# A graph network layer on one core: gathering rows of h in three bf16 parts instead of rows of a first-layer table

## The reference

```python
h = jnp.maximum(_layernorm(x, axis=-1), 0.0)
# layer 0: an MLP over every edge in both directions, summed at the nodes
x_p, x_f = h[src], h[dst]
fwd = concatenate([x_f, x_p, edge_attr], axis=1)      # 80 wide
bwd = concatenate([x_p, x_f, edge_attr], axis=1)
m = relu(concatenate([fwd, bwd]) @ Wf1 + bf1) @ Wf2 + bf2
flow = segment_sum(m, concatenate([dst, src]))         # 64 wide
x = x + relu(flow @ Wn1 + bn1) @ Wn2 + bn2
# layer 1: sum of neighbours
h = jnp.maximum(_layernorm(x, axis=-1), 0.0)
return x + segment_sum(h[dst], src)
```

## Time and profile before

| | |
|---|---|
| median of 3 runs | 9138.04 us |
| profiled execution: span, first to last instruction | 7224.1 us |
| profiled execution: its own time | not given apart from the span |
| start, up to POOL's first gather | 149.8 us |
| edge phase, first gather to last scatter | 149.8 to 4323.8 us |
| busy: POOL, TensorE, VectorE, ScalarE | 5197.9, 4419.8, 3200.3, 1352.3 us |
| mean granted TensorE clock | 0.624 |
| moved by the DMA queue of POOL's DMAs | 183.68 MB in 153824 packets |

### The profile page before, as it was taken

One profiled execution on the slowest core, in us unless ns is written; L12 is line 12 of the kernel. 1 busy time (PEld: TensorE's weight loads), 2 busy tenths in 40 slices (PEclk: granted clock), 3 DMA queues, 4 the chain that ended last, 5 costly groups with the idle time before them and its releaser, 6 DMA issues.

```text
span 7224.1 us, 127054 instructions
## 1 busy us (share of the span) xinstructions
PE 4419.8 (61%) x23241; PEld 3987.8 (55%) x23244; DVE 3200.3 (44%) x15358; ACT 1352.3 (19%) x4288; POOL 5197.9 (72%) x5767
## 2 busy tenths in 40 slices
PE   4666666666666666666666679999733333333333
PEld 3655556555555655555565569999533333333333
DVE  5444444444444444444444466666523232323232
ACT  2222222222222222222222234434200000000000
POOL 2777777777777777777777766666377777777776
PEclk8666676666766666766667785555655555555555
DMA  5222222222222222222222123333111111111111
GB/s 154 43 46 43 43 43 43 43 42 43 42 43 43 42 43 42 42 42 42 43 42 42 41 35 73 71 71 73 30 14 14 14 14 14 14 14 14 14 14 20
DMA packets 1109393, 290.45 MB, mean 40 GB/s; under 512 B 992782, under 2 KB 1058701, under 8 KB 1108518
## 3 DMA queue, kind: packets, MB, share of 16 engines
q0 software_dynamic: 153824, 183.68, 10.7%
q1 hardware_dynamic: 954758, 88.54, 10.3%
q10 hardware_dynamic: 576, 16.16, 0.7%
HBM read 223.49 MB, written 82.32 MB: 42 GB/s over the span
## 4 chain that ended last, share of the span: by engine, by line
POOL 59%; issue 27%; DVE 6%; PE 3%; DVEq 2%; DMA 2%; POOLq 0%; ACT 0%; ACTq 0%; SPq 0%
POOL records L620 21%; POOL ring L674 20%; POOL ring L610 18%; DVE acc L1266 3%; DVEq L331 1%; PE bank L1010 1%; DVE oht L1337 1%; DVE ohd L1337 1%; DVEq L1266 1%; DMA ring<-records 0%; PE bank L943 0%; PE bank L846 0%; DMA row_next<-in_sd 0%; PE bank L944 0%; PE bank L972 0%
## 5 line engine op out<-in xcount | busy, mean ns | idle before, releaser
L620 POOL DMA_INDIRECT records<-rec,pos x1664 | 1650.3, 992 | 526.7 <-issue 507.8
L674 POOL DMA_INDIRECT ring<-h_rows,didx x1568 | 1491.1, 951 | 576.3 <-issue 477.5
L610 POOL DMA_INDIRECT ring<-t_rows,sidx x1568 | 1519.5, 969 | 484.9 <-issue 482.1
L943 PE MATMUL bank<-ring,ident 128*128 x3328 | 1094.3, 431 | 1254.6 <-DMA ring<-t_rows,sidx 1249.8
L943 PEld LDWEIGHTS bank<-ring,ident 128*128 128x128 f32 x3328 | 868.4, 320 | 1309.9 <-issue 1309.8
L1072 PE MATMUL bank<-ring,ohd 128*128 x1664 | 376.2, 402 | 1282.8 <-POOLq L684 1282.2
L1072 PEld LDWEIGHTS bank<-ring,ohd 128*128 128x128 f32 x1664 | 362.9, 330 | 1295.9 <-issue 1295.9
L1275 DVE TENSOR_TENSOR prod<-bank,q_row 128x392 f32<-128x392 f32 x416 | 235.7, 567 | 1895.8 <-PE bank L959 1895.6
L944 PE MATMUL bank<-w,cmb 113*128 113x128 f32 x3328 | 1026.2, 411 | 0.0
L1266 DVE TENSOR_TENSOR acc<-acc,bank 128x65 f32 x3328 | 734.6, 221 | 524.9 <-issue 279.1
L1266 DVE TENSOR_TENSOR xs<-xs,bank 128x32 f32 x1664 | 304.3, 183 | 1384.2 <-PE bank L1072 1371.3
(11 more groups left out here) (213 smaller groups left out, 6508.9 us busy)
## 6 DMA issues: line engine op xcount, KB each, us to landing
ring<-records SPq DMA_DIRECT2D x104, 536.0 KB, 4.3
rec_i<-by_d_sd SPq DMA_DIRECT2D x1664, 1.0 KB
cmb<-by_d_ea SPq DMA_DIRECT2D x1664, 8.0 KB
records<-rec,pos POOLq DMA_INDIRECT x1664
ring<-t_rows,sidx POOLq DMA_INDIRECT x1568
ring<-h_rows,didx POOLq DMA_INDIRECT x1568, 2.4
by_d_ea<-in_ea ACTq DMA_DIRECT2D x8, 1579.0 KB, 19.1
t_rows<-cmb SPq DMA_DIRECT2D x26, 256.0 KB, 2.2
```

The lines of the kernel that those rows point to most:

```text
L610: nc.gpsimd.indirect_dma_start(out=ring[:, m * W + r * U + u, :], out_offset=None, in_=t2_rows, in_offset=bass.IndirectOffsetOnAxis(ap=sid ...
L620: nc.gpsimd.indirect_dma_start(out=records, out_offset=bass.IndirectOffsetOnAxis(ap=pos[:, r, u:u + 1].bitcast(U32), axis=0), in_=rec[:, r ...
L674: nc.gpsimd.indirect_dma_start(out=h2g[:, w * W + t, :], out_offset=None, in_=h2_rows, in_offset=bass.IndirectOffsetOnAxis(ap=didx[:, k, t ...
L943: nc.tensor.matmul(p, ident[:, :], ring[:, bass.ds(at[u], 1), :].rearrange("p a c -> p (a c)"), start=True, stop=False)
```

## The change

The table is no longer made. In its place ScalarE's three bf16 parts of h are written to DRAM as they are (`h3_rows`, 96 bf16 numbers a row, 192 bytes; one DMA). POOL gathers those rows. TensorE turns each gathered tile by a product with the identity (`transpose_sources`, four bf16 products a group), ScalarE copies the result (one more copy of 96 x 512 a group) into the first 96 rows of `cmb`, the expanded dst parts go to a buffer of their own (`cmb_dst`), and `hidden` is now `wdst` times `cmb_dst` plus `wsrc` times `cmb`, both fp32. The wait for the gather moves from `hidden` to `transpose_sources`, which stands half a group earlier. Gathers run LEAD = 4 groups ahead, and a gather stands behind the scatter of its step. In the start the table products leave TensorE's stream, h's parts are made earlier, one of the three reads of each piece of the schedule moves from VectorE to ScalarE, and the second is done once for all four pieces. POOL's first gather no longer waits for the schedule.

```diff
-ring = ring_flat.rearrange("p (t c) -> p t c", c=P)
+hring = ring_flat[:, 0:RG * H3 // 2].bitcast(BF16).rearrange("p (t c) -> p t c", c=H3)
+cmb_dst = rest[0:H3, 0:2 * U * P].rearrange("p (k u n) -> p k u n", k=2, u=U)
@@ SyncE @@
-            rounds_of(sp, NG // 2, store_t2)
-            sp.wait_ge(sched_done, 1)
...
+            load_sources(0, 0)
+            load_sources(1, 1)
+            sp.wait_ge(hi_ready, 1)
+            sp.wait_ge(mid_ready, 1)
+            sp.wait_ge(lo_ready, 1)
+            sp.dma_start(h3_rows.rearrange("(b p) f -> p b f", p=P), h3[:, :, :]).then_inc(h3_written, 16)
+            sp.wait_ge(sched_done, 1)
+            sp.wait_ge(ea_first, 16)
@@ GpSimd @@
-            for k in range(2):
-                pool.wait_ge(t2_written[k], 16 * (NG // 2))
             pool.wait_ge(rearranged, 1)
             nc.gpsimd.memset(cmb[H3:H3 + 1, :, :, :], 1.0).then_inc(ones_set, 1)
-            pool.wait_ge(mid_ready, 1)
             pool.wait_ge(hist_ps, 2)
-            pool.wait_ge(sched_done, 2)
+            pool.wait_ge(h3_written, 16)
...
-                        out=ring[:, m * W + r * U + u, :], out_offset=None, in_=t2_rows,
+                        out=hring[:, m * W + r * U + u, :], out_offset=None, in_=h3_rows,
...
-                        m2, r2 = m + (r + 2) // R, (r + 2) % R
+                        m2, r2 = m + (r + LEAD) // R, (r + LEAD) % R
+                        scatter_records(s * 8 + m, r)
                         if m2 < gathers:
-                            gather_t2(s + m2 // 8, m2 % 8, r2)
-                        scatter_records(s * 8 + m, r)
-            gather_t2(0, 0, 0)
-            gather_t2(0, 0, 1)
+                            gather_h3(s + m2 // 8, m2 % 8, r2)
+            for g in range(LEAD):
+                gather_h3(0, g // R, g % R)
@@ ScalarE @@
-            tables(0, True, False)
             nc.scalar.activation(h3[:, :, 0:D], h, ACT.Copy).then_inc(hi_ready, 1)
-            span(act, 1, 8, tables)
             act.wait_ge(r1_ready, 1)
-            nc.scalar.activation(h3[:, :, D:2 * D], ln_tmp, ACT.Copy).then_inc(mid_ready, 1)
-            span(act, 8, NG // 2 - 1, tables)
+            nc.scalar.activation(h3[:, :, D:2 * D], h, ACT.Copy).then_inc(mid_ready, 1)
...
+                    nc.scalar.activation(base_row[k][:, c * JC:(c + 1) * JC], pb[6][:, 0:JC], ACT.Copy).then_inc(base_copied, 1)
...
+                act.wait_ge(srcT_ps, v)
+                nc.scalar.activation(cmb[0:H3, r, :, :].rearrange("p u n -> p (u n)"), pb[5][0:H3, :], ACT.Copy)
                 act.wait_ge(hd_ps, v)
-                nc.scalar.activation(cmb[0:H3, r, :, :].rearrange("p u n -> p (u n)"), pb[1][0:H3, :], ACT.Copy).then_inc(cmb_ready, 1)
+                nc.scalar.activation(cmb_dst[:, r % 2, :, :].rearrange("p u n -> p (u n)"), pb[1][0:H3, :], ACT.Copy).then_inc(cmb_ready, 1)
@@ TensorE @@
+            def transpose_sources(i, r, gathered):
+                at = four(pe, gs_row, i * W + r * U, RG - 1)
+                if gathered:
+                    pe.wait_ge(gat[r], 16 * U * (i + 1))
+                for u in range(U):
+                    ins = nc.tensor.matmul(pb[5][0:H3, u * P:(u + 1) * P], hring[:, bass.ds(at[u], 1), :].rearrange("p a c -> p (a c)"), ident_h[:, :],
+                                           start=True, stop=True)
+                ins.then_inc(srcT_ps, 1)
...
-                    nc.tensor.matmul(p, ident[:, :], ring[:, bass.ds(at[u], 1), :].rearrange("p a c -> p (a c)"), start=True, stop=False)
-                    ins = nc.tensor.matmul(p, cmb[:, r, u, :], w3[:, :], start=False, stop=True)
+                    nc.tensor.matmul(p, cmb_dst[:, r % 2, u, :], wdst[:, :], start=True, stop=False)
+                    ins = nc.tensor.matmul(p, cmb[:, r, u, :], wsrc[:, :], start=False, stop=True)
@@ VectorE @@
+            dve.wait_ge(hi_ready, 1)
+            nc.vector.tensor_tensor(h, h, h3[:, :, 0:D], ALU.subtract).then_inc(r1_ready, 1)
             digit_one_hots(0)
+            dve.wait_ge(mid_ready, 1)
+            nc.vector.tensor_tensor(h, h, h3[:, :, D:2 * D], ALU.subtract).then_inc(r2_ready, 1)
             digit_one_hots(1)
...
-                    nc.vector.tensor_copy(base_row[k][:, s], pb[6][:, 0:JC])
-                    nc.vector.tensor_scalar(blk[k][:, s], pb[6][0:1, 0:JC], 1.0 / P, None, ALU.mult)
                     nc.vector.tensor_copy(e0f[:, s], pb[7][0:1, HCOL:HCOL + JC]).then_inc(sched_read, 1)
+                dve.wait_ge(base_copied, (n + 1) * (J // JC))
+                own.link(nc.vector.tensor_scalar(blk[k][:, :], base_row[k][0:1, :], 1.0 / P, None, ALU.mult))
```

More of the change, by code:

```diff
@@ L447, in _ @@
             sp.wait_ge(h2_written, 16)
-            for k in range(2):
-                sp.wait_ge(t2_written[k], 16 * (NG // 2))
+            sp.wait_ge(h3_written, 16)
         FB_STEPS = 15
@@ L833, in _ @@
             pe.wait_ge(wflow_ready, 1)
-            def transpose_h(i, k):
-                pe.wait_ge(hs_ready, i * 2 + k + 1)
-                nc.tensor.transpose(pb[k][:, 0:P], hs[:, k, :], ident[:, :]).then_inc(hsT_ready, 1)
-            def tables(i, first, last):
-                for k in range(2):
-                    if not first:
-                        pe.wait_ge(t2s_ready, i * 2 + k - 1)
-                        pe.sem_inc(pe_tick, 1)
-                    pe.wait_ge(hT_ready, i * 2 + k + 1)
-                    for u in range(U):
-                        ins = nc.tensor.matmul(pb[2 + k][:, u * P:(u + 1) * P], hT[:, k, :], w12[:, u, :], start=True, stop=True)
-                    ins.then_inc(tab_ready, 1)
-                if not last:
-                    for k in range(2):
-                        transpose_h(i + 1, k)
             def tile_counts(k):
@@ L879, in _ @@
             nc.tensor.matmul(pb[7][0:NB, 481:482], ident[0:NB + 1, 1:NB + 1], start_col[:, :], start=True, stop=True).then_inc(n_ready, 1)
-            tables(5, False, False)
             tile_counts(1)
-            tables(6, False, False)
-            schedule(1, 0)
-            schedule(1, 1)
-            tables(7, False, False)
-            schedule(1, 2)
-            schedule(1, 3)
-            tables(8, False, False)
+            for c in range(J // JC):
+                schedule(1, c)
             pe.wait_ge(hexp_ready, 1)
@@ L891, in _ @@
                              start=True, stop=True).then_inc(ncol_ps, 1)
-            tables(9, False, False)
             pe.wait_ge(ncol_ready, 1)
@@ L896, in _ @@
             nc.tensor.matmul(pb[7][0:NB, 481:482], upto[0:NB, 0:NB], ncol[:, :], start=True, stop=True).then_inc(n_ready, 1)
-            tables(10, False, False)
             tile_counts(0)
-            tables(11, False, False)
-            schedule(0, 0)
-            schedule(0, 1)
-            tables(12, False, True)
-            schedule(0, 2)
-            schedule(0, 3)
-            pe.wait_ge(t2s_ready, NG)
+            for c in range(J // JC):
+                schedule(0, c)
             q = pb[4][:, 0:(U + 1) * NB].rearrange("p (u b) -> p u b", b=NB)
@@ L1477 @@
     x[0:N] = inputs["x"]
-    w12 = np.zeros((P, U, P), np.float32)
-    for u in range(U):
-        w12[u * D:(u + 1) * D, u, :] = np.concatenate([second, first], axis=1)
-    as_dst = np.concatenate([first, second], axis=1)
+    as_src, as_dst = np.concatenate([second, first], axis=1), np.concatenate([first, second], axis=1)
     twice = np.concatenate([w["bf1"], w["bf1"]])[None, :]
```

133 lines of the change are left out of this document (52 added, 81 removed).

## The result

Five runs of the changed kernel had a median of 9222.14 us (9186.49 to 9224.75), beside 9138.04 us for before (five runs, 9119.58 to 9163.98). The ratio is 1.0075 [1.0052, 1.0097]: 0.75% slower, where 9108 us was predicted with 0.14 for "slower".

What follows compares the result with a forecast made beforehand. POOL's stream of indirect DMAs was taken to bound the edge phase. Steady state 0, start -36 and last groups +6 gave -30 us, from 9138 to 9108 us, own range 9065 to 9167 us (9060 to 9170 us stated with the chances).

Steps and rivals of the forecast that it cites:

- What bounds the kernel now: Edge phase: POOL's stream of indirect DMAs fills it, 10.3 us a group; TensorE's 3.2 us wait for gathers is slack.
- the sum: Whole kernel: 0 - 36 + 6 = -30 us; span 7194 us, median 9108 us, the 1913.9 us outside the span unchanged.
- Part 1: Edge phase, steady state: added products and copy stay under POOL's 10.3 us a group, so they cost nothing.
- TensorE's round: Edge phase: 7.1 us a group without its wait, 7.7 us with the products, 8.3 us with the copy too.
- TensorE was the bound: Rival, edge phase: the wait at L943 is true loss, round falls 10.3 to 8.3 us, 8324 us; chance 0.03.
- dearer gathers: Rival, edge phase: gathers into a bf16 ring cost POOL more, each 10 ns adding 16 us; 9190 us, chance 0.12.
- The price of a gather: POOL, edge phase: 192-byte bf16 rows cost the present 969 ns, change 0; ends -18 and +23 ns, -28 and +36 us.
- Part 2, the start: Start of the kernel: first scatter at 136.4 instead of 167.62 us, four more gathers behind it; gain 36 us (25 to 45).
- The eight pieces of the schedule: Start, VectorE: 1.6 us each, 12.8 us plus twice 1.0 us, instead of 28.9 us; saves 14.1 us.
- that step: Start: without table products in TensorE's stream VectorE goes on at 87.5 us, 9.1 us earlier (bounds 7 and 13).
- Part 3, the last groups: Last 24 groups, without gathers: products partly show and the last gathered group is further back, +6 us (0 to +18).
- The rule of the Trainium skill: DMA of rows under 512 bytes: less than full rate, gathers' data later, but POOL free as soon and the sum unchanged.

Runs made afterwards that it cites:

- after_c: The changed kernel (after), unchanged, run again on an occasion without pauses: 7213.12 us, 0.9985 [0.9975, 0.9994] of before; profile span 7209.6 us.
- before_again: The kernel before, unchanged, profiled once more: 9133.96 us, with a span of 9132.3 us.
- part D: Blocks 73 to 103 of after, in a kernel of four versions: added products and copy kept, POOL's gathers left out (old rows): 6.8 us a group.
- after_src_early: After, with the four added products two groups ahead at the round's end and ScalarE's copy behind its last: 7218.34 us, 0.9995 of before, without pauses.
- before_two_loads: Before, with SyncE's eight loads of a group made into two of the same bytes: 7226.63 us, one run, without pauses.
- after_no_src: After, without the four added products and ScalarE's copy of them past the first four groups: 7213.94 us, 0.9991 of before, without pauses.

## Why the prediction was wrong, point by point

- **The step that failed** is the first: "What bounds the kernel now", with its end in the sum, "No view shows what lies in the 1913.9 us between the span and the median of the runs; I take it as unchanged". The 1914 us were in the edge phase and the last one, where the timed runs pause. In them POOL waits for positions, 3.9 us a group, and the stream of DMAs, from which the cover of the added work was worked out ("Both are under POOL's 10.3 us, so POOL's stream is the cover and the cost is nothing"), is not the bound: a group takes 14.2 us. A span 21% under the median of the runs was the warning; the page was then of an execution unlike the timed ones.
- **Part 1, "the cost is nothing".** Right where POOL bounds (10.26 us a group, after_c). In the result's profile block 1 to 96 took 5406.9 us against 5292.3 us in before_again: +114.6 us, 0.30 us a group. The term missing was the added work on a round that nobody covers; taken away on one chip it is worth 211 us. Of the 89 us between these two spans the start gives back 33.5 and the last groups 8, and behind the last scatter after is 16 us longer, for which I have no cause.
- **TensorE's round** was put at 7.1 us, and 7.7 to 8.3 us with the added work, by taking its wait off POOL's 10.3 us. Without gathers it is 5.9 us in before and 6.8 us in after (part D). The margin under POOL was larger than foreseen, and in the timed runs it was no margin.
- **The rival that was nearest**, "TensorE was the bound", had 0.03 and the wrong sign: it let the change gain the wait for gathers. That wait was slack; what a bound on TensorE's side does is let the added work show. The slower rival that I did price (dearer gathers, 0.12) was refuted: 972 against 969 ns, and 969 ns in after_c. That after came out slower at all, 0.14 in the forecast, came by another way than the one priced.
- **The price of a gather**, taken as 0 with ends of -18 and +23 ns: right.
- **Part 2, the start.** First gather foreseen at 91 to 98 us, first scatter at 136.4 us; measured 95.51 and 139.54 us (95.06 and 139.10 in after_c). Against 167.62 us in the earlier trace rows that is 28 us, foreseen 31; the other profiles with the start of before have their first scatter between 162 and 170 us, so the gain is known to a few us only. The eight pieces of the schedule come 1.70 us apart, not 1.6, and VectorE went on at 89.0 us (after_c; 89.5 in after), not 87.5. The reading behind that step was wrong: the wait for TensorE did not go with the table products, it is 7.33 us against 7.64, and TensorE's 100 histogram products last 8.87 us (L793) against 4.98 (L824). VectorE is merely done earlier, at 81.7 us instead of 88.95. This gain is real with pauses as well: from block 1 (191.9 against 225.4 us) after is 33.5 us ahead, then loses it.
- **Part 3, the last groups**, foreseen as +6 (0 to 18): in after_c block 96 to the last scatter took 220.4 us, in the first profile of before 209.0: +11.4 us. The added products show in full there (6.5 against 5.8 us a group, above).
- **The sum where its premise holds.** Against the first profile of before, after_c gains 33.6 us up to block 96 (foreseen 36), gives back 11.4 in the last groups, and 8 us after the last scatter, where I foresaw 0: 14.5 us less span, foreseen 30. Timed, -11 us [-18, -4]. Of the latter 8 us I have no cause; 5 of them lie between the last scatter and the first gather of the last phase, 905 against 900 us, which before's own profiles have at 897 to 900.

The rule of the Trainium skill that was weighed ("DMA: Bandwidth & Descriptors", Specifications: less than full rate under 512 bytes) would have had later data and no change of the sum. The write of the 192-byte rows took 17.1 us, between the 13.2 us that rows and the 20 us that bytes would give by the earlier trace rows:

```profile
h_rows<-h SPq DMA_DIRECT2D x1, 2496.0 KB, 17.1
```

2496 / 17.1 = 146 GB/s, counted as there, no less than for rows of 128 bytes (126): no run here shows the rule's penalty.

**What stays open.** What makes TensorE's hand-overs late, and so how much of the loss with pauses is the products, the copy or the hand-over, and whether after_src_early wins there. One more engine is held up: SyncE. Its register moves at L397, which wait for nothing, last 29 ns and at most 37 in the first profile of before (1000 to 3000 us), but up to 724 ns in before_again; the register instructions of TensorE, ScalarE, VectorE and POOL keep their time there (at most 81 ns). Whether SyncE's loads come late enough to matter is not shown, and before_two_loads, which could have told, ran without pauses. Another mark goes with the pauses: the trace of before in the first profile has 155,291 semaphore updates, that of before_again 59,004; after_c 161,261, after 61,596. So an execution with pauses also leaves fewer records. The Trainium skill ("NOTIFIC — the notification-queue block", Overflow: three behaviours, one of which stalls the engine) says that a full queue of records can either lose records or hold up the engine that writes them. Each of the two would fit one mark, the lost records or the late engines; that a queue of records is behind either, no run here shows.

## What to carry to other kernels

Compare the profile's span with the median of the timed runs before reading any bound from it: where they differ by as much as here (21%), the profile shows an execution that the metric does not have, and its slack may not exist. Work that is free behind one engine's stream is worth bounding for the case in which that stream is not the bound: here 0 us where POOL covers it, 211 us where it does not. Several versions in one kernel, each over a stretch of the same loop, compare in one execution what separate runs on changing machines cannot.

## What was not expected of the hardware

- The same chip ran before in 9024 us and, later, in 7230 us. With pauses the instructions of the compute engines keep their length (a ScalarE copy 592 ns in both); only what TensorE hands to ScalarE and VectorE comes late, by some 6 us in the timeline above. What ScalarE hands to TensorE takes 0.29 us with pauses and without.

- With the change TensorE's granted clock is lower where POOL bounds, and the amount of work alone does not explain it. 2000 to 3000 us of the first profile of before, of after_c and of after_src_early:

```profile
2000.00:3000.00 1000.00, 673.51 (x3705) 587.01 (x3705) 449.91 (x2134) 228.52 (x583) 762.94 (x779) 0.69 0.21 42
```

```profile
2000.00:3000.00 1000.00, 797.13 (x4100) 711.44 (x4099) 450.60 (x2152) 287.26 (x682) 762.41 (x780) 0.51 0.18 27
```

```profile
2000.00:3000.00 1000.00, 727.23 (x4076) 631.59 (x4075) 447.05 (x2134) 285.86 (x679) 763.53 (x777) 0.68 0.19 26
```

In after_c 11% more products are 18% more busy time, at 0.51 of full speed (nearly the lower level, 1.2 GHz) against 0.69, and no time is lost, since TensorE waits for POOL anyway. After_src_early has the same products in another place of the round and 0.68; after_no_src has as few products as before and 0.58. So the clock goes here with the order of TensorE's work and waits within the round too, and not with its amount alone.
